# Cross-attention on one core, with the scores also computed keys-on-partitions and q and k stacked as high/low parts

## The reference

```python
q = layernorm(x) @ Wq.T + bq;  k = ctx @ Wk.T + bk;  v = ctx @ Wv.T + bv      # 16 heads of 16
scores = where(mask == 0, -1e9, q.k / 4);  attn = softmax(scores)             # (2, 16, 1024, 77)
x = x + (attn @ v) @ Wo.T + bo
xn = layernorm(x);  logits = xn @ w_router;  gate, eidx = top_k(softmax(logits), 2)
# each token goes to slot p of expert e for both its experts; expert_in (8, 768, 256)
h = relu(expert_in @ w1 + b1);  y = h @ w2 + b2
x = x + sum_k gate_k * y[expert_k, slot_k]
```

## Time and profile before

| | us |
|---|---|
| median of 3 runs (556.15 to 558.66) | 557.07 |
| span of the profiled execution | 548.5 |
| stage A, start to the first transpose of stage B | 244.3 |
| last residual of stage A (macro 7) | 219.9 |
| stage B | 304.2 |

### The profile page before, as it was taken

The page is one execution under the profiler, slowest core; times in us unless marked ns, Lnnn a source line. Parts: engine busy times, 40 slices in busy tenths (PEclk is TensorE's granted clock), DMA queues, the critical chain, the costliest instruction groups (busy, mean ns, idle before and its releaser), DMA issues.

```text
span 548.5 us, 11698 instructions
## 1 busy us (share of the span) xinstructions
PE 449.6 (82%) x3845; PEld 431.5 (79%) x3845; DVE 343.4 (63%) x817; ACT 306.0 (56%) x738; POOL 240.6 (44%) x357
## 2 busy tenths in 40 slices
PE   3766719788797785209999999999999999999990
PEld 3655618777686775209999999999999999999990
DVE  2788899899999996303663655545556456364430
ACT  2367817666767762206765547757456576554520
POOL 2524273536455335642133625626446365362531
PEclk9979968799989987557999999999999999999996
DMA  8997031201111111222231433514414343131110
GB/s 253 283 198 244 1 104 52 77 0 39 38 39 39 41 40 40 78 81 65 97 111 34 157 113 81 178 43 154 134 39 150 108 141 119 35 88 40 47 40 0
DMA packets 36668, 49.62 MB, mean 90 GB/s; under 512 B 5350, under 2 KB 31377, under 8 KB 36501
## 3 DMA queue, kind: packets, MB, share of 16 engines
q1 hardware_dynamic: 27277, 34.03, 21.9%
q0 software_dynamic: 6144, 12.64, 6.9%
q10 hardware_dynamic: 3208, 2.45, 1.4%
HBM read 34.33 MB, written 18.96 MB: 97 GB/s over the span
## 4 chain that ended last, share of the span: by engine, by line
PE 65%; DVE 12%; issue 7%; DMA 6%; POOL 5%; ACT 3%; POOLq 0%; DVEq 0%; ACTq 0%
PE ps L1062 19%; PE ps L1064 18%; PE ps L1063 18%; DMA xs<-in_x 4%; PE ps L1164 3%; PE ps L1284 2%; DVE ptl L818 2%; DVE xn L974 2%; POOL expert_in L503 2%; DMA expert_in<-shared,sidx 1%; ACT pb L628 1%; DVE o L838 1%; PE ps L1110 1%; DVE xs L987 1%; PE ps L1176 1%
## 5 line engine op out<-in xcount | busy, mean ns | idle before, releaser
L729 ACT ACTIVATE shared<-ps,bcol 128x256 f32<-128x256 f32 x192 | 80.4, 470 | 100.6 <-PE ps L1064 100.2
L1062 PE MATMUL ps<-xTh,wh 128*128 128x256 f32 x416 | 119.6, 287 | 0.5 <-DVE xTl L791 0.5
L1063 PE MATMUL ps<-xTl,wh 128*128 128x256 f32 x416 | 118.8, 286 | 0.0
L1006 DVE TENSOR_TENSOR hl<-shared,hh 128x512 fp32r<-128x512 f32 x96 | 66.7, 695 | 81.0 <-ACT hh L735 81.0
L1062 PE MATMUL ps<-wh,hh 128*128 128x256 f32 x384 | 110.5, 288 | 0.0
L1064 PE MATMUL ps<-xTh,wl 128*128 128x256 f32 x384 | 109.1, 284 | 0.0
L1064 PE MATMUL ps<-wh,hl 128*128 128x256 f32 x384 | 108.6, 283 | 0.0
L1063 PE MATMUL ps<-wl,hh 128*128 128x256 f32 x384 | 107.9, 281 | 0.0
L547 POOL DMA_INDIRECT out<-shared,ctok x48 | 51.2, 1067 | 100.1 <-DVE shared L1028 83.9
L539 POOL DMA_INDIRECT shared<-out,ctok x48 | 70.2, 1463 | 38.3 <-issue 17.9
L1062 PEld LDWEIGHTS ps<-xTh,wh 128*128 128x128 f32 x416 | 80.4, 193 | 0.9 <-issue 0.9
(11 more groups left out here) (143 smaller groups left out, 869.1 us busy)
## 6 DMA issues: line engine op xcount, KB each, us to landing
wraw<-in_L_ffn_w SPq DMA_DIRECT2D x16, 1024.0 KB, 5.4
expert_in<-zrow SPq DMA_DIRECT2D x6, 1032.0 KB, 20.1
shared<-expert_in SPq DMA_DIRECT2D x24, 258.0 KB, 2.8
out<-xs SPq DMA_DIRECT2D x4, 512.0 KB, 2.9
xs<-in_x ACTq DMA_DIRECT2D x1, 1792.0 KB, 17.4
b_b<-in_L_ffn_b SPq DMA_DIRECT2D x1, 1024.0 KB, 19.2
shared<-out,ctok POOLq DMA_INDIRECT x48, 2.9
out<-shared,ctok POOLq DMA_INDIRECT x48, 2.5
```

The source lines that it names most:

```text
L729: ins = a.activation(hf[:, i % 2, s * CH:(s + 1) * CH], ps[:, i, s * CH:(s + 1) * CH], ACT.Relu, bias=bcol[:, bass.ds(at(e * MT + 2 * i + ...
L1006: v.tensor_tensor(hl[:, par, 2 * i * CH:2 * (i + 1) * CH], hf[:, i % 2, :], hh[:, par, 2 * i * CH:2 * (i + 1) * CH].bitcast(F32), ALU.subt ...
L1062: T.matmul(dst, sh, mh, start=first, stop=False)
L1063: T.matmul(dst, sh, ml, start=False, stop=False)
```

## The change

Stage A is rewritten; stage B computes the same with the same instructions, only its buffers are allocated anew.

- q and k are stored per head as 48 rows: high, high, low parts of q (`qs`) against high, low, high parts of k (`kst`), two heads (96 rows) in one operand, with k block-wise zero. One float32r matmul then does what three did. To get that layout, q and k go through DRAM: SP stores two arrays and loads six (`bounce_q`, once a macro) or twelve (k).
- Scores are computed twice. `scores` gives them with tokens on partitions, only for the maximum, four calls a macro of 4 heads x 2 tiles, each over 4 x 78 columns. `scores_t` gives them with 78 keys on partitions and 256 tokens in columns, for one pair of heads a call, eight calls a macro; the mask and the negated maximum (transposed on PE and held as two bf16 parts) come in by a second, bf16 matmul with a selector. The exponential of that is already transposed.
- The exponential is taken twice from PSUM on ACT, once as f16 (`phi`) and once as float32 (`pf`); the low half `plo` is their difference, six times a macro on DVE and twice on POOL.
- `project_q` and the output projection are plain float32 matmuls, 4 each a macro instead of 12; the high/low splits of x and o go away. `bo` enters as a bf16 matmul, so POOL's addition `xbo` goes away. The second normalization goes from DVE to ACT, which writes both copies of the row at once.
- An iteration now holds: units of macro i, scores and maxima of macro i+1, q of macro i+2, the output of macro i-1, routing of macro i-2. The loop is unrolled.
- SP issues the zero rows after q of macros 0 and 1, and the weights of expert 0 after q of macro 2. Expert 0's halves are made at the end of stage A (ACT, then DVE), expert 1's weights are loaded after the last residual.

The core of the diff:

```diff
+            def bounce_q(m):
+
+                sp.wait_ge(S["q_rest"], m + 1)
+                if m >= 2:
+                    sp.wait_ge(S["qs_loaded%d" % (m % 2)], 16 * NLD * (m // 2))
+                sp.dma_start(qscr[m % 2, 0].rearrange("(r p) t -> p r t", p=P), qh[:].bitcast(F32)).then_inc(S["q_stored"], 16)
+                sp.dma_start(qscr[m % 2, 1].rearrange("(r p) t -> p r t", p=P), ql[:].bitcast(F32)).then_inc(S["q_stored"], 16)
+                sp.wait_ge(S["q_stored"], 32 * (m + 1))
+                if m >= 2:
+                    sp.wait_ge(S["b_ready"], NG * (m - 1))
+                for par in range(2):
+                    for c, part in enumerate((0, 0, 1)):
+                        at0 = par * SR + c * DH
+                        sp.dma_start(qs[at0:at0 + DH, m % 2].bitcast(F32),
+                                     qscr[m % 2, part].rearrange("(j s d) t -> s d j t", s=2, d=DH)[par]
+                                     ).then_inc(S["qs_loaded%d" % (m % 2)], 16)
...
+            bounce_q(0)
+            bounce_q(1)
+            sp.wait_ge(S["zrow_ready"], 1)
+            xz = xe[0:SLOTS, :].rearrange("(p r) d -> p (r d)", p=P)
+            for i in range(SLOTS // P // 8):
+                sp.dma_start(xz[:, i * 8 * XW:(i + 1) * 8 * XW].rearrange("p (r d) -> p r d", d=XW),
+                             zrow[:].unsqueeze(1).to_broadcast([P, 8, XW])).then_inc(S["zero_done"], 16)
+            bounce_q(2)
+            load_weights(0, 0)
+            load_weights(0, 1)
+            bounce_q(3)
...
+            def exps(m, q):
...
+                a.activation(phi[:, m % 2, hs, :], src.rearrange("p (h t) -> p h t", h=2), ACT.Exp)
...
+                a.activation(pf[:, u % 4, :], src, ACT.Exp).then_inc(S["exp_done"], 1)
...
+            def maximum(m, p):
...
+                v.tensor_reduce(nm[:, :, 4 * p:4 * p + 4],
+                                ps[:, SC:SC + 2, 0:4 * KV].rearrange("p t (h k) -> p t h k", k=KV), AX.X,
                                 ALU.max, negate=True).then_inc(S["max_ready"], 1)
...
+            def rest_p(m, q):
...
+                v.tensor_tensor(plo[:, m % 2, hs, :], pf[:, u % 4, :].rearrange("p (h t) -> p h t", h=2),
+                                phi[:, m % 2, hs, :], ALU.subtract).then_inc(S["lo_dve"], 1)
...
+                    T.matmul(dst, identb[:], mb[:, (m % MPB) * G + t, :].unsqueeze(1).to_broadcast([P, 4, KV]),
+                             start=True, stop=False)
+                    for j in range(2):
+                        pr = 2 * p + j
+                        ins = T.matmul(ps[:, SC + t, j * 2 * KV:(j + 1) * 2 * KV], qs[:, m % 2, pr, ts],
+                                       kst[:, b, 2 * pr:2 * pr + 2, :].rearrange("p h k -> p (h k)"),
+                                       start=False, stop=(j == 1))
...
+            def scores_t(m, q):
...
+                if u >= 2:
+                    pe.wait_ge(S["exp_done"], u - 1)
+                cs = slice((m % MPB) * GT, (m % MPB + 1) * GT)
+                for s in range(2):
+                    dst = ps[0:KV, ST + q % 2, s * GT:(s + 1) * GT]
+                    T.matmul(dst, kst[:, b, 2 * q + s, :], qs[:, m % 2, q, :], start=True, stop=False)
+                    ins = T.matmul(dst, ek_sel[:, 2 * q + s, :], mmx[:, cs], start=False, stop=True)
+                ins.then_inc(S["b_ready"], 1)
...
+            for i in range(NM + 2):
+                f, w, n = i + 2, i - 1, i - 2
+                units, nxt, front, tail, slots = i < NM, i + 1 < NM, f < NM, 0 <= w < NM, n >= 0
+                if units:
+                    scores_t(i, 0)
+                if nxt:
+                    scores(i + 1, 0)
+                if front:
+                    turn_xn(f)
+                if units:
+                    scores_t(i, 1)
+                if nxt:
+                    scores(i + 1, 1)
+                if tail:
+                    times_v(w, 0)
+                if units:
+                    scores_t(i, 2)
+                if front:
+                    project_q(f)
+                if units:
+                    scores_t(i, 3)
+                if nxt:
+                    scores(i + 1, 2)
+                if slots:
+                    turn_x2(n)
+                if tail:
+                    times_v(w, 1)
+                if units:
+                    scores_t(i, 4)
+                if units:
+                    scores_t(i, 5)
...
+                if nxt:
+                    scores(i + 1, 3, (lambda: logits(n)) if slots else None)
+                elif slots:
+                    logits(n)
+                if tail:
+                    turn_o(w)
+                if units:
+                    scores_t(i, 6)
+                if nxt:
+                    turn_max(i + 1)
+                if units:
+                    scores_t(i, 7)
+                if tail:
+                    project_o(w)
+                if slots:
+                    positions(n)
```

More of the change, by code:

```diff
@@ L92, in xattn_moe_kernel @@
     SLOTS = NE * CAP
+    KV = NK + 1
+    NP = NH // 2
+    SR = 3 * DH
+    SK = 2 * SR
+    MROW = 96
     VW = 3 * DH + 1
[L94 to L95 removed]
+    VS = 64
+    NG = NH // 2
+    PAIRS = 4
+    POOL_LO = 2
     x_v = x.rearrange("b (t p) d -> p (b t) d", p=P)
@@ L521, in tags @@
+            picks(NM - 1)
+            dispatch(NM - 1)
             def tags(c, par, half):
@@ new lines, in positions @@
+            def positions(n):
+                pe.wait_ge(S["run_ready"], n + 1)
+                for t in range(G):
+                    dst = ps[:, SC + 1, LG_AT + t * NE:LG_AT + (t + 1) * NE]
+                    T.matmul(dst, before[:], ohs[:, t, :], start=True, stop=False)
+                    ins = T.matmul(dst, onesb[:], run[:, t, :], start=False, stop=True)
+                ins.then_inc(S["pos_ready"], 1)
+            pe.wait_ge(S["const_ready"], 1)
+            pe.wait_ge(S["wk_loaded"], 16)
@@ L1190, in positions @@
-            def positions(n, bank_no):
-                pe.wait_ge(S["run_ready"], at(n + 1))
-                for t in range(G):
-                    dst = ps[:, bank_no, t * NE:(t + 1) * NE]
-                    T.matmul(dst, before[:], ohs[:, t, :], start=True, stop=False)
-                    ins = T.matmul(dst, onesb[:], run[:, t, :], start=False, stop=True)
-                ins.then_inc(S["pos_ready"], 1)
-            project_k()
-            turn_xn(0)
-            bias_rows()
-            pe.wait_ge(S["w2_loaded"], at(16 * 2))
@@ new lines, in _ @@
+            ins.then_inc(S["k_projected"], 1)
+            turn_xn(0)
+            pe.wait_ge(S["wv_loaded"], 16)
+            turn_weight(2, 5, "wv_turned")
+            pe.wait_ge(S["wq_copied"], 1)
+            project_q(0)
+            pe.wait_ge(S["mask_ready"], 1)
+            pe.wait_ge(S["const_ready"], 2)
+            for t in range(TPB):
+                ins = T.transpose(bank16(2)[0:KV, t * P:(t + 1) * P], mb[:, t, :], identb[:])
+            ins.then_inc(S["mask_turned"], 1)
+            pe.wait_ge(S["wv_copied"], 1)
@@ new lines, in _ @@
+            for b in range(NB):
+                for k in range(KT):
+                    ins = T.matmul(ps[0:KV, 0, b * D:(b + 1) * D], cT[:, k, b, :], wvT[:, k, :],
+                                   start=(k == 0), stop=(k == KT - 1))
+            ins.then_inc(S["v_projected"], 1)
+            pe.wait_ge(S["wo_loaded"], 16)
+            turn_weight(3, 1, "wo_turned")
+            turn_xn(1)
+            project_q(1)
+            pe.wait_ge(S["kst_loaded"], 16 * 12)
+            pe.wait_ge(S["vf_ready"], 1)
```

1427 lines of the change are left out of this document (715 added, 712 removed).

## The result

The changed kernel takes 614.6 us (median of four runs, 605.0 to 617.1) where the kernel before takes 556.7: a ratio of 1.0925, 95% interval 1.0875 to 1.0975. The forecast was 554 us, and its range ended at 573. Two of the four runs fell in a slower state of the chip, which the ratio leaves out and the medians keep: the loss is 51.5 us by the ratio and 58 us by the medians. The profiled execution is the fastest of the four, 605.0 us with a span of 603.0.

A forecast was written before the change was run, and what follows sets the result against it. Before, DVE bound stage A and TensorE stage B; after, the chain through the q bounce sets the macro. Last residual at 215.1, tail 26, stage B from 241.1, span 545.3, plus 8.6: 554 us, range 534 to 573.

The forecast's parts named there:

- The window, 15.4 by hand: Stage A iteration, from q's loads landed to the last scores_t: followed step by step, done at 15.4 us.
- half clock after each stand: Rival, PE becomes the bound: narrow float32r near 0.3 us, half clock after stands 0.6 a macro; 575 us, chance 0.08.
- my 0.15: Score matmuls on PE: float32r of 156 columns taken at 0.15 us each, 16 a macro.
- Plain float32: Plain float32 matmuls on PE: 0.6 us each at the low clock from L1094, 0.3 to 0.6 in the loop.
- the term that the prediction had added: DVE's rest_p beside POOL's two-input steps: 0.5 us a macro added, making 20.7 us.
- The rival's 2.0 us more an iteration: Rival, DVE and POOL hold each other: 2.0 us more in iterations 1 to 7, 568 us, chance 0.20.
- The bounce, 4.8: q's loads between iterations: 0.1 wait, 1.9 for six issues, 2.8 for the last to land, 4.8 us.
- The start: Before the loop: q(2) queued behind zero rows issued at 32 us and drained at 63; scores(2) at 69.
- this is the largest single loss: At the start, PE stands some 20 us waiting for q(2) behind the zero rows.
- The other rival, that q overtakes the zero rows: Rival, the bounce isn't held: scores(2) at 54 us, not 69; 539 us, chance 0.17.
- The last iterations, 45: End of stage A: iterations 6, 7 and 8 take 15.6, 15.3 and 14.1 us, last residual at 215.1.
- Around the span: Time outside the span: 557.07 less 548.5, 8.6 us, added to the span of 545.3.

The follow-up runs named there:

- e5: Kernel of e1 with unread matmuls on PE, 16 where it waits for x2T and 24 where it waits for divide_o: 569.9 us, ratio 1.0226.
- e1: Changed kernel with a third buffer for q, loads waiting for scores_t of the macro before: 586.4 us, ratio 1.0527.
- e14: Changed kernel, still with two q buffers, with the unread matmuls of e5: 606.6 us, ratio 1.0872.
- e6: Kernel of e1 with wqT, woT, xT and oT as float32r, both projections in one pass, low parts left out: 574.5 us, ratio 1.0340.
- e9: Changed kernel with all four edits (third q buffer, unread matmuls, two moves of order, spread fills): 563.2 us, ratio 1.0124.
- e2: Changed kernel with zero rows later in SP's list: q(2), three fills, q(3), three fills, then weights: 613.4 us, ratio 1.0967.
- e3: Kernel of e1 with the zero rows moved as in e2: 586.3 us, ratio 1.0531.
- e8: Kernel of e1 with SP's list spread, at most two fills or one load ahead of any q: 575.7 us, ratio 1.0369.
- e7: Kernel of e1 with divide_o(w, 1) ahead of maximum(i+1, 3) on DVE and head_q(f) ahead of exps(i, 3) on ACT: 582.9 us, ratio 1.0471.

## Why the prediction was wrong

Reckoned by its own terms, in the profiled execution:

| term | predicted | measured |
|---|---|---|
| scores(2, 0) starts | 69 | 78.9 |
| macro, scores(2) to scores(7) | 20.2 | 27.1 |
| window / bounce in iteration 3 | 15.4 / 4.8 | 20.4 / 7.6 |
| iterations 6, 7, 8 | 45.0 | 60.5 |
| last residual | 215.1 | 275.0 |
| tail | 26 | 28.6 |
| stage B | 304.2 | 299.4 |
| around the span | 8.6 | 2.0 |

What failed is the price of the macro, 20.2 us where 27.1 were measured: its window was worked out with TensorE at the high clock, and its bounce from a load of another shape. The chain was the right one: PE waits for q's loads in every macro, DVE is at 58 to 63% and no longer the bound, and the miss in the span, 57.7 us, is 9.9 of start, 34.6 of macros, 15.5 of the last iterations and 2.6 of tail, less 4.8 of stage B, whose cause isn't known (the same 2400 matmuls, busy 283.6 us in place of 288.4). The sizes failed, in these steps.

*The window, 15.4 by hand.* Against the trace of iteration 3, in us from its start: second maximum done 3.8 predicted, 5.2 measured; high half of q 8.4, 10.3; maximum 3 done 13.4, 15.1; `split_max` 14.1, 17.3; `scores_t` 7 15.4, 20.4. I had followed PE at the high clock throughout. The granted clock is 0.50 in the first 3.7 us, behind the wait for q, and 0.50 again behind the wait for `divide_o`. PE's sum was small too: 13 us a macro predicted, 22 busy at a clock of 0.68, and still some 15.7 at 1.00 (e5's 18.2 to 18.5 us less 2.6 to 2.7 of unread matmuls). Of the 5.0 us missed 1.9 lie ahead of the high half of q, 1.3 between it and `split_max`, where `divide_o` stands (below), and 1.8 from there to the last `scores_t`, 3.1 us in place of 1.3. e5, with the clock at 1.00, takes 2.9 us off the macro of e1; for the changed kernel itself e14 doesn't show such a gain, so how the 5.0 us split between the clock and the rest is argued here and not measured. The prediction named the mechanism ("half clock after each stand") with 0.6 us a macro and a chance of 0.08, tied to narrow float32r matmuls near 0.3 us. These were not slow: two of 156 columns take under 0.29 us with the mask's start behind them (L1208 at 139.52, L1204 at 139.81), so my 0.15 stood at the high clock; at the low one two take 0.54 us (131.42 to 131.96).

*Plain float32.* Priced from L1094, 0.6 us each at the low clock, which has 154 columns; the projections have 256. Four at the high clock take 1.54 us (L1186, 0.39 each), inside my 0.3 to 0.6, but those of `project_o` run at the low one, two in 2.0 us (L1273), 1.0 each. They weren't in the window as I saw it, since `project_o` lies beside the bounce. Both together are worth 11.9 us in the kernel of e1 (e6).

*DVE beside POOL.* In this macro `divide_o` took 1.87 us where its median is 0.42, beside POOL's `rest_p` (L906 and L479 above), 1.45 us more, on the path. The Trainium skill, "GPSIMD Engine Reference", § Specifications, has the two engines contend over SBUF when VectorE reads two SBUF inputs; these rows agree, and so does POOL's 3.04 us scatter of e9. Taken for every such step it would be too strong: `rest_p` on DVE has a median of 0.68 us over 48. Over the seven iterations from 79 to 275 us `divide_o` and DVE's `rest_p` together lie 3.8 us above their medians, 0.5 us an iteration: just the term that the prediction had added. The rival's 2.0 us more an iteration, with its 0.20 and 568 us, isn't there.

*The bounce, 4.8.* Six loads of 16 partitions are issued over 2.69 us, not 1.9, and the last lands 4.9 us after its issue, where I took the 2.8 of a chunk load: 7.6 us in place of 4.8. I had a row of another shape and gave it no range. e1 shows that more hangs on the bounce than its length beyond `project_o`: PE is idle for 1.9 us of it, and the macro loses 4 (27.7 to 23.7), because the stand and the low clock behind it go too.

*The start.* The queue's reckoning held: 39.9 plus 31 us of drain is 71, and q(2) was stored by 71.5. Its loads then took 7.4 us and not 5. The zero rows began 7.9 us later than reckoned, because k was split at 16.1 us and not at 12.5, and because q(1) had to be waited for and its stores took longer. That "this is the largest single loss" is refuted. Macro 0's iteration was to be done at 49 us, but q(2) is ready only at 60, so PE stands 10.8 us and not 20. e2 and e3 took the fills away and gained nothing, as what follows in the queue then hits q(4); e8, which spreads them, gained 10.7. The other rival, that q overtakes the zero rows, is refuted by the same rows.

*The last iterations, 45.* Iteration 6 took 23.8 us for 15.6, iteration 7 took 19.8 for 15.3 and iteration 8 16.9 for 14.1. They were priced at the high clock too; the windows of the last two show 0.60 and 0.50, with PE busy 16.6 and 11.3 us. In e5, at 0.90 and 0.70, they take 17.5 and 17.3 us: in iteration 7 the loss goes with the clock, while for iteration 8 no run shows that it does.

*Around the span.* The 8.6 us came from a median less a profiled span, of different executions; in one execution it is 2.0 us. That error made the forecast larger, not smaller. From the profiled 605.0 to the median 614.6 there are 9.6 us of which no trace tells.

By the ratios 51.5 us were lost. Of these 22 are shown to go with the q bounce (e1; 28 by the medians, 21 between the two profiled runs); of what is left after that, each edit taken alone, 17 go with the low clock (e5), 9 with SP's order (e8) and 3, barely shown, with two places in the lists (e7). All four together gave 45 of the 51 that they add up to (51.4 of 58.9 by the medians). In their place the first dispatch, q(4) and iterations 7 and 8 become late in one kernel or another; that these make up the difference isn't shown.

## What to carry to other kernels

A transfer that is on the path of every iteration costs more than its own length: it leaves TensorE standing, and here the steps behind the stand ran at half the clock. So price every TensorE step behind a stand at both levels, and look at the granted clock of the window that the change will leave, not of the one that it removes. And a wait that is taken out of a queue is only gone when what is queued behind it has been followed to its own deadline: here it came back at q(4), then at the first dispatch.

## What the hardware showed that I hadn't expected

- 40 unread bfloat16 matmuls of 128 columns a macro made the kernel 16.5 us faster (586.4 to 569.9): granted clock 0.78 before, 1.00 with them. 64 ahead of the longest wait gave no such gain, because the scores behind them started 2.2 us later and the clock fell at the next stand.
- Work taken from PE can lower its clock: one-pass projections saved 11.9 us on e1 but 5 on e9, where the clock from residual 0 to 5 was 0.86 against 0.97 and the stretch got 4.0 us longer.
- A DMA's issue itself can be held on SP: a store of q took 0.38 us to issue in most macros and 1.99 behind the zero rows; the bias broadcast took 8.6.
- A POOL scatter of 0.98 us took 3.04 beside DVE's 2048-column subtraction of two SBUF tensors.
